# A mixture-of-experts kernel whose results are added to the output's rows by accumulating scatters instead of being gathered at the end

## The chip, the core and the metric

The kernel runs on one core of a Trainium2 chip. The core has five engines that run side by side and are ordered by semaphores: TensorE (matmuls), VectorE, ScalarE, GpSimd and SyncE, which here only issues transfers. Sixteen DMA engines move the data. Transfers issued by SyncE and ScalarE go through a hardware queue; transfers with a list of row numbers ("indirect" transfers) are issued by GpSimd, whose own program writes their descriptions.

The metric is the time of one execution on the device, in microseconds. Before the change the median of three runs is 848.52 us (847.52 to 849.83).

## What is computed

The input is 32 batches of 256 tokens with 128 numbers each, 8192 rows in all. Each row is normalised; the result goes through a causal attention of 16 heads of 8 numbers, with projection, residual and a second normalisation, and through a mixture of 8 experts, of which each token uses its best two. Both results are added to the input.

```python
def ffn(x, Wr, W1, b1, W2, b2):              # E = 8 experts, D = 128, H = 512, K = 2
    probs = softmax(einsum('bsd,ed->bse', x, Wr))
    topv, topi = top_k(probs, 2)
    combine = sum(topv[..., None] * one_hot(topi, 8), axis=2)
    for each expert e:
        h = gelu(x @ W1[e] + b1[e])
        out += combine[..., e] * (h @ W2[e] + b2[e])
    return out

xn = layernorm(x)
result = x + attention(xn, w_qkv, w_proj, b_proj, gamma, beta) + ffn(xn, Wr, W1, b1, W2, b2)
```

## The kernel before the change

The 8192 rows are held as `NT = 64` tiles of 128 rows in `x_all`; two tiles are one batch. The program has four parts.

**The beginning.** The input is loaded, its moments are computed, each row is normalised into `xn_rows`, and the router's scores are formed. VectorE picks two experts for each row and computes a slot for each of the two picks: the picks are sorted by expert, each expert's run is padded to a multiple of `S = 256` slots, and there are `NS = 72` tiles of 256 slots. A slot row in the scratch tensor `x_slots` holds the 128 numbers of the normalised row and a few extra columns: the weights, the first expert's number, and the row of the result. Slots that stay empty hold a row number far out of range (`NOWHERE`).

**The attention steps.** Batches run through a pipeline of five stages (PROJECT, MAXIMA, SOFT, FINISH, LAST); step `s` works on batch `s` in the first stage, on `s - 1` in the second, and so on, so there are 36 steps. The table `USES` gives the order of the work within a step, and each engine follows it in its own program. Most steps run in a hardware loop of two steps per pass; the last ones are written out, since they also load and convert the weights of the experts (`pieces`, L416). What matters here is SyncE's order within a step: it loads the second half of a batch's queries and keys (`load_half`, L437 and L438), stores the projected queries and keys of the next batch (L462), loads that batch's first half, and, when ScalarE has made `shift_T`, writes four rows of shifts into `q_diag` (L478). Then the next step's second half follows. TensorE waits for the second half ahead of its use `m6`. GpSimd masks the probabilities and sends, a few tiles per step, the rows to their slots (`send_tile`, L572, 128 scatters of 128 rows). The last stage (`last`, L957) adds the attention's result to the batch's rows in `x_all` and raises `res_ready`.

**The expert tiles.** Each of the 72 tiles takes three steps. SyncE loads the tile's 256 slots into one of four buffers `xg` (L497). TensorE transposes them (L1236), multiplies by the first weights (L1259, `wide`) and two tiles later by the second (L1250); ScalarE applies the activation (L687) and finally multiplies the result by the token's weight into one of four buffers `y` (L714). GpSimd scatters it, two scatters of 128 rows per tile (L619), to the rows given by `dest`: pick `c` of row `t` goes to row `2t + c` of the scratch tensor `parts_dram`, rows of empty slots go to spare rows behind. `placed[k]` counts the landings of tile `k` modulo 8. ScalarE waits for the landing of the tile four back before it writes a `y` buffer again (L710), VectorE for the one eight back before it writes `dest` again (L1021). All engines but SyncE run this stage as a loop of eight tiles, with the experts of the eight packed into one register.

**The end.** When all scatters have landed (L502), SyncE loads both parts of each row, in eight chunks of 1 MB (L507); VectorE adds them to each other and to `x_all` (L1072, L1074); ScalarE's queue stores the eight chunks of the output (L740).

Of the kernel before, what the change touches and what calls it, by code (L numbers as in the profile page):

```python
# [5 lines left out]
F32 = mybir.dt.float32  # L6
# [8 lines left out]
P = 128  # L15


def attention_and_moe(nc, x, w_qkv, w_proj, b_proj, gamma, beta, w_router, w1, b1, w2, b2, out):
# [18 lines left out]
    SW = D + 5  # L37
# [6 lines left out]
    with ctx:  # L44
# [10 lines left out]
        parts_dram = nc.dram_tensor("parts_dram", [2 * B * T + NS * S, D], F32).ap()  # L55
# [101 lines left out]
        Y_BUFS, DEST_BUFS = 4, 8  # L157
        y = o_T[:, :, :].rearrange("p b (t d) -> p b t d", d=D)
        spare_row = sb("spare_row", [P, NS * 2])
        dest = sb("dest", [P, DEST_BUFS, 2], I32)  # L160
        chosen = sb("chosen", [P, DEST_BUFS, 2, 2])
        LAST_CHUNKS, PART_BUFS = 8, 4
        LC = NT // LAST_CHUNKS
        parts = xn_rows[:, :, :].rearrange("p t d -> p (t d)")[:, 0:NT * D].rearrange("p (b t d) -> p b t d", b=PART_BUFS, d=2 * D)
# [68 lines left out]
        parts_loaded = [sem(f"parts_loaded{u}") for u in range(PART_BUFS)]  # L233
        parts_added = sem("parts_added")
        out_ready = sem("out_ready")
        out_stored = sem("out_stored")
# [70 lines left out]
        def steps(eng, step, after=((), ()), first_tile=None, written_out=False):  # L307
# [3 lines left out]
            first_whole = STAGES - 1 if not written_out else TAIL  # L311
# [95 lines left out]
        def _(sp):  # L407
# [31 lines left out]

            def step(s, par):  # L440
# [39 lines left out]
            sp.wait_ge(consts, 25)  # L480
            step(0, 0)
            sp.wait_ge(consts, 28)
            steps(sp, step)


            for u in range(2):
                sp.wait_ge(sent[u], 32 * (NT // 2))
# [23 lines left out]
        def _(pool):  # L511
# [28 lines left out]
            pool.iota(xn_rows[:, :, D + 1], pattern=[[2 * P, NT]], base=0, channel_multiplier=2,  # L540
                      allow_small_or_imprecise_dtypes=True).then_inc(consts, 1)
            pool.memset(xn_rows[:, :, D + 3], 1.0).then_inc(consts, 1)
            pool.iota(minus_row[:, :], pattern=[[0, 1]], base=0, channel_multiplier=-1,
                      allow_small_or_imprecise_dtypes=True).then_inc(consts, 1)
            pool.iota(spare_row[:, :], pattern=[[P, NS * 2]], base=2 * B * T, channel_multiplier=1,
                      allow_small_or_imprecise_dtypes=True).then_inc(consts, 1)


            pool.memset(fill[:, :, :], 0.0).then_inc(consts, 1)
            pool.wait_ge(consts, 24)  # L550
            pool.memset(fill[:, :, D + 1], NOWHERE).then_inc(fill_ready, 1)
            pool.memset(q_diag[:, 0, :, :, :], 0.0).then_inc(consts, 1)
            for c, (begin, end) in enumerate(MOMENTS):
# [6 lines left out]
                elif c == 2:  # L560
                    pool.memset(v_aug[:, :, :, :, :], 0.0).then_inc(consts, 1)
                    pool.wait_ge(consts, 27)
                    pool.memset(v_aug[:, :, :, :, HD:HD + 1], 1.0).then_inc(consts, 1)
# [6 lines left out]
            def send_tile(t):  # L570
                for c in range(2):
                    pool.indirect_dma_start(out=x_slots, out_offset=bass.IndirectOffsetOnAxis(ap=slot_i[:, t, c:c + 1], axis=0),  # L572
                                            in_=xn_rows[:, t, :], in_offset=None).then_inc(sent[t % 2], 16)
# [48 lines left out]
            tiles(pool, tile, load=False)  # L622


        @block.scalar
        def _(act):
# [68 lines left out]
            def tile(s, k, experts):  # L695
# [10 lines left out]
                if second(s):  # L706
# [3 lines left out]
                    later(act, placed[before], (s - k) * 4 + (32 if k >= 2 + Y_BUFS else 0), beyond(s, 1 + Y_BUFS))  # L710
                    act.wait_ge(xg_used, s * 2 - 2)
                    act.wait_ge(y_filled, s - 1)
                    for t in range(2):
                        act.activation(y[:, of % Y_BUFS, t, :], bank[("head", "maxB")[par]][:, D * t:D * (t + 1)], ACT.Copy,  # L714
                                       scale=chosen[:, of, t, 0:1]).then_inc(y_ready, 1)
# [22 lines left out]
            for c in range(LAST_CHUNKS):  # L738
                act.wait_ge(out_ready, c + 1)
                act.dma_start(out.rearrange("b (t p) d -> p (b t) d", p=P)[:, LC * c:LC * (c + 1), :],  # L740
                              x_all[:, LC * c:LC * (c + 1), :]).then_inc(out_stored, 16)
            act.wait_ge(out_stored, 16 * LAST_CHUNKS)


        @block.vector
        def _(dve):
            V = nc.vector
            dve.wait_ge(consts, 23)
# [87 lines left out]
            def places():  # L836
# [3 lines left out]
                then(V.tensor_scalar(xn_rows[:, :, D + 4], best[:, 0, :], -1.0, float(E), ALU.mult, ALU.add))  # L840
# [165 lines left out]
            def tile(s, k, experts):  # L1006
                quad = k % 4
                par = quad % 2
                if first(s):
# [3 lines left out]
                    V.scalar_tensor_tensor(out=chosen[:, k, :, :], in0=xg[:, quad, :, D + 4:D + 5].to_broadcast([P, 2, 2]),  # L1013
# [304 lines left out]
```

## Time and profile before the change

| | |
|---|---|
| median of three runs | 848.52 us |
| the profiled execution | 851.77 us |
| its span, first to last instruction | 850.0 us |
| TensorE busy | 699.9 us (82%) |
| VectorE busy | 692.9 us (82%) |
| ScalarE busy | 525.4 us (62%) |
| GpSimd busy | 536.0 us (63%) |
| moved by the DMA engines | 93.66 MB, 110 GB/s in the mean |

The profile comes from one execution. It lists each instruction with its start and its length, the idle time ahead of it, and what ended that idle time ("<-"). "issue" stands for idle time in which the engine waited for nothing that the profile shows. PE is TensorE, DVE VectorE, ACT ScalarE, POOL GpSimd; SPq and ACTq are transfers issued by SyncE and ScalarE. A line number such as L619 is one of the kernel. The ends of matmuls are modelled, so that a busy TensorE isn't TensorE at its peak. The shares over the whole span are means over stages with different limits; the rows further down are read by stage.

### The profile page before, as it was taken

To read this page: it belongs to the slowest core of one execution; us is meant where nothing else is said; L and a number is where in the kernel's file an instruction comes from. 1 tells how busy PE (TensorE), PEld (TensorE's weight loads), DVE (VectorE), ACT (ScalarE), POOL (GpSimd) and SP (SyncE) were. 2 spreads that over 40 slices of the span, in tenths; PEclk is the share of its full clock that TensorE was granted. 3 is DMA by queue.
4 is the path that set the end of the run, shared out by engine and by line. 5 is a ranking of instruction groups with operands and counts; after the bars stand their busy time and mean duration, and the time that the engine had idled before them with its cause. 6 is when DMAs were issued, how large, how long until landed. Compare 5 with 4: busy or idle time off the path is not lost.

```text
span 850.0 us, 24989 instructions
## 1 busy us (share of the span) xinstructions
PE 699.9 (82%) x7877; PEld 518.1 (61%) x7878; DVE 692.9 (82%) x1617; ACT 525.4 (62%) x1039; POOL 536.0 (63%) x575
## 2 busy tenths in 40 slices
PE   1366579999999999999888888868999999999800
PEld 1243346666666666666655555537888889888800
DVE  5778878898999998989889999557788888888744
ACT  4541346565656565656556565537989999999800
POOL 8750456767676776767777777334767676667710
PEclk9999899999999999999999999978999999999955
DMA  8294122232323232232233432202222222222189
GB/s 220 80 400 122 64 84 94 81 111 79 114 77 111 80 111 94 94 98 90 84 127 107 139 125 78 64 7 62 84 85 80 85 88 84 82 82 82 56 266 335
DMA packets 113313, 93.66 MB, mean 110 GB/s; under 512 B 16618, under 2 KB 97650, under 8 KB 113268
## 3 DMA queue, kind: packets, MB, share of 16 engines
q1 hardware_dynamic: 95508, 70.26, 27.0%
q0 software_dynamic: 8704, 18.17, 5.9%
q10 hardware_dynamic: 9056, 4.66, 1.9%
q8 instruction: 25, 0.41, 0.2%
q14 instruction: 20, 0.16, 0.1%
HBM read 43.85 MB, written 48.93 MB: 109 GB/s over the span
## 4 chain that ended last, share of the span: by engine, by line
PE 56%; DVE 13%; issue 7%; POOL 7%; DMA 6%; ACT 5%; SPq 5%; DVEq 0%; ACTq 0%; POOLq 0%
PE wide L1259 10%; PE bank_head L1148 7%; PE wide L1113 5%; PE bank_head L1250 5%; PE bank_maxB L1250 5%; PE bank_maxA L1127 4%; PE bank_maxB L1127 3%; DMA xn_rows<-parts_dram 3%; DMA k_cat<-qk_rows 3%; DVE shift L911 3%; POOL probs L581 3%; PE bank_misc L1173 3%; SPq L478 2%; PE bank_maxB L1131 2%; PE bank_maxA L1131 2%
## 5 line engine op out<-in xcount | busy, mean ns | idle before, releaser
L581 POOL TENSOR_SCALAR_AFFINE_SELECT probs<-probs 128x512 f32<-128x512 f32 (+1 forms) x192 | 158.3, 833 | 103.6 <-ACT probs L653 102.8
L653 ACT ACTIVATE probs<-wide 128x1024 f32<-128x1024 f32 x192 | 188.8, 1018 | 47.3 <-PE wide L1117 24.5
L619 POOL DMA_INDIRECT parts_dram<-o_T,dest x144 | 161.0, 1118 | 74.7 <-issue 48.6
L572 POOL DMA_INDIRECT x_slots<-xn_rows,slot_i x128 | 127.3, 995 | 62.8 <-DVE slot_i L868 31.4
L911 DVE TENSOR_REDUCE shift<-bank_maxA 128x2 f32<-128x512 f32 (+1 forms) x192 | 132.1, 688 | 20.1 <-PE bank_maxA L1131 12.9
L911 DVE TENSOR_REDUCE shift<-bank_maxB 128x2 f32<-128x512 f32 (+1 forms) x192 | 131.5, 685 | 4.9 <-PE bank_maxB L1131 0.8
L687 ACT ACTIVATE probs<-wide,b_all 128x256 f32<-128x256 f32 x288 | 121.4, 478 | 16.8 <-PE wide L1259 10.0
L1148 PE MATMUL bank_head<-probs,v_aug 128*32 128x256 f32 (+1 forms) x2048 | 98.9, 334 | 19.1 <-POOL probs L581 18.9
L1259 PE MATMUL wide<-xgT_raw,xnT 128*128 128x256 f16 x864 | 109.2, 277 | 3.7 <-DVE xgT_raw L1020 3.6
L1003 DVE TENSOR_TENSOR probs<-probs 128x512 f16<-128x512 f32 x144 | 99.7, 692 | 5.5 <-ACT probs L693 1.1
L1127 PE MATMUL bank_maxA<-k_cat,q_diag 128*128 128x128 f16 (+1 forms) x512 | 76.2, 252 | 28.5 <-DVE shift L911 19.5
L1148 PEld LDWEIGHTS bank_head<-probs,v_aug 128*32 128x32 f32 x2048 | 60.5, 111 | 56.2 <-issue 21.4
L1259 PEld LDWEIGHTS wide<-xgT_raw,xnT 128*128 x864 | 78.8, 99 | 16.4 <-issue 4.9
L671 ACT ACTIVATE o_T<-bank_head 128x512 f32<-128x512 f32 x64 | 38.2, 597 | 73.8 <-PE bank_head L1148 73.8
L1113 PE MATMUL wide<-q_diag,k_cat 128*128 128x512 f16 x256 | 76.9, 384 | 0.0
L1127 PE MATMUL bank_maxB<-k_cat,q_diag 128*128 128x256 f16 (+1 forms) x512 | 75.5, 250 | 0.3
L1127 PEld LDWEIGHTS bank_maxA<-k_cat,q_diag 128*128 128x128 f16 x512 | 36.7, 98 | 56.2 <-DVE shift L911 34.4
L1127 PEld LDWEIGHTS bank_maxB<-k_cat,q_diag 128*128 128x128 f16 x512 | 42.2, 99 | 30.3 <-DVE shift L911 8.0
L1131 PE MATMUL bank_maxB<-mask,ident 128*128 128x256 f16 (+1 forms) x192 | 60.5, 315 | 0.0
L1131 PE MATMUL bank_maxA<-mask,ident 128*128 128x256 f16 (+1 forms) x192 | 60.4, 314 | 0.0
L1250 PE MATMUL bank_head<-xnT,probs 128*128 x864 | 55.3, 220 | 0.0
L1250 PE MATMUL bank_maxB<-xnT,probs 128*128 x864 | 55.0, 219 | 0.2 <-DVE probs L1003 0.2
(174 smaller groups left out, 1252.4 us busy)
## 6 DMA issues: line engine op xcount, KB each, us to landing
qk_rows<-split SPq DMA_DIRECT2D x32, 512.0 KB, 3.2
x_slots<-fill SPq DMA_DIRECT2D x16, 598.5 KB, 7.6
fill<-x_slots SPq DMA_DIRECT2D x72, 133.0 KB
q_diag<-qk_rows SPq DMA_DIRECT2D x256, 32.0 KB
k_cat<-qk_rows SPq DMA_DIRECT2D x64, 128.0 KB
xn_rows<-parts_dram SPq DMA_DIRECT2D x8, 1024.0 KB, 11.8
x_all<-in_x SPq DMA_DIRECT2D x8, 512.0 KB, 7.6
pieces_f<-in_w SPq DMA_DIRECT2D x8, 512.0 KB, 4.8
```

The costliest lines, as they stand in the source:

```text
L572: pool.indirect_dma_start(out=x_slots, out_offset=bass.IndirectOffsetOnAxis(ap=slot_i[:, t, c:c + 1], axis=0), in_=xn_rows[:, t, :], in_of ...
L581: pool.affine_select(out=part, in_=part, compare_op=ALU.is_ge, fill=0.0, base=0, pattern=[[0, n], [1, P]], channel_multiplier=-1).then_inc ...
L619: pool.indirect_dma_start(out=parts_dram, out_offset=bass.IndirectOffsetOnAxis(ap=dest[:, of, t:t + 1].bitcast(U32), axis=0), in_=y[:, of ...
L653: act.activation(probs[:, u, :], ps[:, :], ACT.Exp, scale=SCALE).then_inc(empty, 1)
L687: act.activation(hT[:, par, c, :], wide[par][:, S * c:S * (c + 1)], ACT.Gelu, bias=b1_all[:, bass.ds(e, 1), c:c + 1].rearrange("p a b -> p ...
L911: V.tensor_reduce(dst, ps[:, :].rearrange("p (j k) -> p j k", j=nh), axis=AX.X, op=ALU.max, negate=True).then_inc(empty, 1)
L1113: last = M(ps[:, 512 * h2:512 * (h2 + 1)], keys[:, gs[0], :], q_diag[:, par, gs[0], 2 * h2:2 * h2 + 2, :], start=True, stop=True)
L1127: M(ps[:, keys * n_:keys * (n_ + 1)], q_diag[:, 1 - par, g, j, P * qt:P * (qt + 1)], k_cat[:, 1 - par, g, 0:keys], start=(n_ == 0), stop=F ...
L1131: M(dst, ident16[:, :], mask16[:, :].rearrange("p (o k) -> p o k", o=1).to_broadcast([P, nh, P]), start=False, stop=True, skip_group_check ...
L1148: last = M(dst, v_aug[:, of, kt, J * g + j, :], p_, start=(kt == 0), stop=(kt == 1), skip_group_check=True)
L1250: last = M(results[:, D * t:D * (t + 1)], hT_parts[:, par, hp, c, P * t:P * (t + 1)], w2_parts[:, wp_, bass.ds(e_2, 1), c, :].rearrange("p ...
L1259: last = M(wide[par][:, S * c:S * (c + 1)], w1_parts[:, wp_, bass.ds(e_1, 1), P * c:P * (c + 1)].rearrange("p a d -> p (a d)"), xgT[:, par ...
```

## The change

The scratch tensor `parts_dram` and the whole end are gone. The output itself is the place where the results meet:

- In the attention steps SyncE stores each batch's finished rows of `x_all` (input plus attention) to the output, at the end of the step after the one that finished them (`begin_out`). The last two batches are stored between the first loads of the expert tiles. GpSimd waits for all 32 stores before its first scatter of results.
- GpSimd's scatters of results carry an addition: each row is added to the output's row in memory. The row number is now that of the token, and empty slots, whose number is out of bounds, are left out by the scatter's bounds check.
- Two scatters that add to the same row must not be in flight together. Within one expert no row occurs twice. So SyncE clears each tile for GpSimd: it waits until the tile's results are in `y`, and, where the tile is the first of a new expert, until the scatters of the three tiles before it have landed. Whether the expert changes is read from the packed experts by register arithmetic. SyncE issues the load of the tile five ahead before it clears a tile.
- A slot row has one extra column less (`SW = D + 4`), since row number and pick need no choice; VectorE's selection shrinks accordingly, and `dest` is a plain copy. The counts in `placed` begin at 16, since the first scatters into `x_slots` are counted there.
- SyncE's loop of attention steps begins two steps later (`in_loop = STAGES + 1`).

```diff
-    SW = D + 5
+    SW = D + 4
...
-        parts_dram = nc.dram_tensor("parts_dram", [2 * B * T + NS * S, D], F32).ap()
+        out_rows = out.rearrange("b t d -> (b t) d")
...
+            def begin_out(b):
+
+                sp.wait_ge(res_ready, b * QT + QT)
+                sp.nop(nofuse=True)
+                sp.dma_start(out[bass.ds(b, 1), :, :].rearrange("a (t p) d -> p (a t) d", p=P),
+                             x_all[:, bass.ds(b * QT, QT), :]).then_inc(out_begun, 16)
+
+            def stores(s):
+
+                return 0 <= s - 1 - LAST < B - 2 if isinstance(s, int) else True
...
                         sp.dma_start(q_diag[row:row + 1, 1 - par, :, j, :], shift_T[G * j:G * (j + 1), :]).then_inc(shift_loaded, 16)
+                if stores(s):
+                    begin_out(s - 1 - LAST)
...
-            def tile(s, k, experts):
-                quad = k % 4
-                if not first(s):
-                    return
-
+            def load_slots(s, quad):
                 later(sp, xg_used, s * 2 - 6, beyond(s, 3))
                 sp.nop(nofuse=True)
                 sp.dma_start(xg[:, quad, :, :], x_slots[bass.ds(s * S, S), :].rearrange("(t p) d -> p t d", p=P)).then_inc(xg_loaded[quad], 16)
...
-            tiles(sp, tile, load=False)
-
-            for u in range(DEST_BUFS):
-                sp.wait_ge(placed[u], 32 * (NS // DEST_BUFS))
-            both = parts_dram[0:2 * B * T, :].rearrange("(t p c) d -> p t (c d)", p=P, c=2)
-            for c in range(LAST_CHUNKS):
-                if c >= PART_BUFS:
-                    sp.wait_ge(out_ready, c - PART_BUFS + 1)
-                sp.dma_start(parts[:, c % PART_BUFS, :, :], both[:, LC * c:LC * (c + 1), :]).then_inc(parts_loaded[c % PART_BUFS], 16)
-
+            EVEN = sum((E - 1) << BITS * j for j in range(0, FIELDS - 1, 2))
+            ODD = sum((E - 1) << BITS * j for j in range(1, FIELDS - 1, 2))
+
+            def changes_at(i):
+
+                experts = experts_of(sp, i)
+                steps_up = (experts >> BITS) - (experts & (EVEN + ODD))
+                return (steps_up & EVEN) + EVEN, (steps_up & ODD) + ODD
+
+            def clear(u, i, k, changes):
+
+                sp.wait_ge(y_ready, u * 2 + 2)
+                sp.nop(nofuse=True)
+                if beyond(u, 0):
+                    bit = BITS * (k + 1)
+                    whole = (changes[k % 2] >> bit - 5 if bit > 5 else changes[k % 2] << 5 - bit) & 32
+                    for back in range(1, Y_BUFS):
+                        if beyond(u, back - 1):
+                            sp.wait_ge(placed[(k - back) % DEST_BUFS], whole + (i * 32 + (FIRST if k >= back else FIRST - 32)))
+                            sp.nop(nofuse=True)
+                sp.nop(nofuse=True).then_inc(cleared, 1)
+
+            AHEAD = 5
+            for s in range(AHEAD):
+                load_slots(s, s % 4)
+                if s in (1, 2):
+                    begin_out(B - 3 + s)
+            changes = changes_at(0)
+            for k in range(UNROLL):
+                load_slots(k + AHEAD, (k + AHEAD) % 4)
+                clear(k, 0, k, changes)
+            with sp.Fori(0, NS // UNROLL - 2) as i:
+                changes = changes_at(i + 1)
+                for k in range(UNROLL):
+                    load_slots(i * UNROLL + (UNROLL + k + AHEAD), (k + AHEAD) % 4)
+                    clear(i * UNROLL + (UNROLL + k), i + 1, k, changes)
...
-                    pool.wait_ge(y_ready, s * 2 - 2)
+                    pool.wait_ge(cleared, s - 1)
                     pool.nop(nofuse=True)
                     for t in range(2):
-                        pool.indirect_dma_start(out=parts_dram, out_offset=bass.IndirectOffsetOnAxis(ap=dest[:, of, t:t + 1].bitcast(U32), axis=0),
-                                                in_=y[:, of % Y_BUFS, t, :], in_offset=None).then_inc(placed[of], 16)
-
+                        pool.indirect_dma_start(out=out_rows, out_offset=bass.IndirectOffsetOnAxis(ap=dest[:, of, t:t + 1].bitcast(U32), axis=0),
+                                                in_=y[:, of % Y_BUFS, t, :], in_offset=None, bounds_check=B * T - 1, oob_is_err=False,
+                                                compute_op=ALU.add).then_inc(placed[of], 16)
+
+            pool.wait_ge(out_begun, 16 * B)
             tiles(pool, tile, load=False)
+            for u in range(DEST_BUFS):
+                pool.wait_ge(placed[u], 32 * (NS // DEST_BUFS) + FIRST)
...
-            for c in range(LAST_CHUNKS):
-                act.wait_ge(out_ready, c + 1)
-                act.dma_start(out.rearrange("b (t p) d -> p (b t) d", p=P)[:, LC * c:LC * (c + 1), :],
-                              x_all[:, LC * c:LC * (c + 1), :]).then_inc(out_stored, 16)
-            act.wait_ge(out_stored, 16 * LAST_CHUNKS)
...
-                    V.tensor_tensor(dest[:, k, :], chosen[:, k, :, 1], spare_row[:, bass.ds(s * 2, 2)], ALU.min).then_inc(xg_used, 1)
+                    V.tensor_copy(dest[:, k, :], xg[:, quad, :, D + 1]).then_inc(xg_used, 1)
```

## Rows read from the trace of the kernel before

**Rows 1.** Busy times by stage: stretch, length, each engine, PEclk, DMA share, GB/s.

```profile
core 0: us, PE busy (x) PEld busy (x) DVE busy (x) ACT busy (x) POOL busy (x), PEclk, DMA share, GB/s
130.00:402.00 272.00, 266.14 (x2884) 175.44 (x2883) 248.34 (x546) 168.28 (x234) 196.60 (x235) 1.00 0.29 94
580.00:802.00 222.00, 215.60 (x2793) 197.35 (x2790) 182.04 (x488) 203.07 (x559) 154.92 (x138) 1.00 0.27 82
812.00:850.00 38.00, 0.00 (x0) 0.00 (x0) 19.60 (x16) 0.00 (x0) 0.00 (x0) 0.50 1.02 331
```

**Rows 2.** The chain that ended last, near its end: start, length in us, what.

```profile
809.34 2.22 DMA parts_dram<-o_T,dest
```

**Rows 3.** Timeline of the last tiles and the end: start, length, engine, line, work.

```profile
804.16 0.63 ACT L714 ACTIVATE o_T<-bank_head,chosen 128x128 f32<-128x128 f32 x2 [0.44 <-PE bank_head L1250]
...
805.54 0.96 POOL L619 DMA_INDIRECT parts_dram<-o_T,dest  x1 [0.99 <-ACT o_T L714]
...
809.34 0.96 POOL L619 DMA_INDIRECT parts_dram<-o_T,dest  x1 [0.30 <-issue]
811.64 19.88 SPq L507 DMA_DIRECT2D xn_rows<-parts_dram  x8
...
819.99 26.82 ACTq L740 DMA_DIRECT2D out<-x_all  x8
```

**Rows 4.** Instructions on `x_slots`, SyncE's queue in the expert stage: ns min/median/max.

```profile
L497 SPq DMA_DIRECT2D fill<-x_slots x72: 368/373/1512, 546.3 to 788.2; - x72
L497 SPq MOVE fill<-x_slots x64: 29/29/29, 587.0 to 788.1; - x64
```

**Rows 5.** The chain that ended last, expert stage: the same matmuls eight tiles apart.

```profile
652.08 1.33 PE wide L1259 x12
...
677.52 1.33 PE wide L1259 x12
```

**Rows 6.** Timeline of a tile in the expert stage: GpSimd's scatters and VectorE's CAST.

```profile
795.97 0.96 POOL L619 DMA_INDIRECT parts_dram<-o_T,dest  x1 [0.44 <-issue]
...
797.23 1.30 POOL L619 DMA_INDIRECT parts_dram<-o_T,dest  x1 [0.30 <-issue]
...
797.74 0.43 DVE L1001 CAST probs<-probs 128x512 f16<-128x512 f32 x1
...
798.97 0.96 POOL L619 DMA_INDIRECT parts_dram<-o_T,dest  x1 [0.44 <-issue]
```

**Rows 7.** Groups of instructions by line: count, busy us, mean ns, idle before.

```profile
L619 POOL DMA_INDIRECT parts_dram<-o_T,dest x144 | 161.0, 1118 | 74.7 <-issue 48.6 <-ACT o_T L714 26.2
L572 POOL DMA_INDIRECT x_slots<-xn_rows,slot_i x128 | 127.3, 995 | 62.8 <-DVE slot_i L868 31.4 <-issue 31.1 <-ACT probs L653 0.3
```

**Rows 8.** Waits on SyncE's queue: who, for whom, us in total, times, longest.

```profile
SPq L496 <- DVE dest L1023: 192.4, 68, 14.6
```

**Rows 9.** Timeline of SyncE's queue in the attention steps.

```profile
305.12 2.44 SPq L478 DMA_DIRECT2D q_diag<-shift_T  x4
307.74 1.72 SPq L437 DMA_DIRECT2D q_diag<-qk_rows  x4
309.50 0.43 SPq L438 DMA_DIRECT2D k_cat<-qk_rows  x1
...
423.96 0.43 SPq L438 DMA_DIRECT2D k_cat<-qk_rows  x1
```

**Rows 10.** Timeline of TensorE in the attention steps, the matmuls of `m6`.

```profile
311.98 0.39 PE L1127 MATMUL bank_maxA<-k_cat,q_diag 128*128 128x128 f16 x4
...
426.45 0.40 PE L1127 MATMUL bank_maxA<-k_cat,q_diag 128*128 128x128 f16 x4 [1.11 <-DMA k_cat<-qk_rows]
...
443.12 0.40 PE L1127 MATMUL bank_maxA<-k_cat,q_diag 128*128 128x128 f16 x4 [1.81 <-DMA k_cat<-qk_rows]
```

**Rows 11.** Timeline of SyncE's queue in a step that also loads a weight piece.

```profile
435.79 0.44 SPq L416 DMA_DIRECT2D pieces_f<-in_w  x1
436.34 3.61 SPq L437 DMA_DIRECT2D q_diag<-qk_rows  x4
440.00 0.42 SPq L438 DMA_DIRECT2D k_cat<-qk_rows  x1
```

**Rows 12.** GpSimd's DMA queue: packets, MB, share of 16 engines' span.

```profile
q0 software_dynamic: 8704, 18.17, 5.9%
```

More of the change, by code:

```diff
@@ L157, in attention_and_moe @@
         Y_BUFS, DEST_BUFS = 4, 8
+        FIRST = 16
         y = o_T[:, :, :].rearrange("p b (t d) -> p b t d", d=D)
-        spare_row = sb("spare_row", [P, NS * 2])
         dest = sb("dest", [P, DEST_BUFS, 2], I32)
[L161 to L164, printed above, removed]
+        chosen = sb("chosen", [P, DEST_BUFS, 2])
         wide = [ctx.enter_context(nc.psum_tensor(f"wide{i}", [P, 1024], F32)) for i in range(2)]
@@ L232, in attention_and_moe @@
         placed = [sem(f"placed{u}") for u in range(DEST_BUFS)]
[L233 to L236, printed above, removed]
+        out_begun = sem("out_begun")
+        cleared = sem("cleared")
         PROJECT, MAXIMA, SOFT, FINISH, LAST = range(5)
@@ L305, in beyond, with steps @@
             return s > n if isinstance(s, int) else True
-        def steps(eng, step, after=((), ()), first_tile=None, written_out=False):
+        assert STAGES % 2 == 1
+        def steps(eng, step, after=((), ()), first_tile=None, written_out=False, in_loop=STAGES - 1):
             experts = None
-            first_whole = STAGES - 1 if not written_out else TAIL
+            first_whole = in_loop if not written_out else TAIL
             count = TAIL - first_whole
@@ L478, in step @@
                         sp.dma_start(q_diag[row:row + 1, 1 - par, :, j, :], shift_T[G * j:G * (j + 1), :]).then_inc(shift_loaded, 16)
-            sp.wait_ge(consts, 25)
+                if stores(s):
+                    begin_out(s - 1 - LAST)
+            sp.wait_ge(consts, 23)
             step(0, 0)
-            sp.wait_ge(consts, 28)
-            steps(sp, step)
+            sp.wait_ge(consts, 26)
+            steps(sp, step, in_loop=STAGES + 1)
             for u in range(2):
-                sp.wait_ge(sent[u], 32 * (NT // 2))
+                sp.wait_ge(sent[u], 32 * (NT // 2 - DEST_BUFS // 4))
+            for u in range(DEST_BUFS):
+                sp.wait_ge(placed[u], FIRST)
             sp.wait_ge(packing, EXPERTS_PACKED)
-            def tile(s, k, experts):
-                quad = k % 4
-                if not first(s):
-                    return
+            def load_slots(s, quad):
                 later(sp, xg_used, s * 2 - 6, beyond(s, 3))
@@ L510, in _ @@
+            changes = changes_at(NS // UNROLL - 1)
+            for u in range(NS - UNROLL, NS):
+                if u + AHEAD < NS:
+                    load_slots(u + AHEAD, (u + AHEAD) % 4)
+                clear(u, u // UNROLL, u % UNROLL, changes)
         @block.gpsimd
@@ L572, in send_tile @@
                     pool.indirect_dma_start(out=x_slots, out_offset=bass.IndirectOffsetOnAxis(ap=slot_i[:, t, c:c + 1], axis=0),
-                                            in_=xn_rows[:, t, :], in_offset=None).then_inc(sent[t % 2], 16)
+                                            in_=xn_rows[:, t, :], in_offset=None).then_inc(placed[2 * t + c] if t < DEST_BUFS // 2 else sent[t % 2], 16)
             def mask(s, u):
@@ L709, in tile @@
                     before = (k - 2 - Y_BUFS) % DEST_BUFS
-                    later(act, placed[before], (s - k) * 4 + (32 if k >= 2 + Y_BUFS else 0), beyond(s, 1 + Y_BUFS))
+                    later(act, placed[before], (s - k) * 4 + (32 + FIRST if k >= 2 + Y_BUFS else FIRST), beyond(s, 1 + Y_BUFS))
                     act.wait_ge(xg_used, s * 2 - 2)
@@ L747, in _ @@
             V = nc.vector
-            dve.wait_ge(consts, 23)
+            dve.wait_ge(consts, 21)
             V.tensor_reduce(is_edge[:, :], head_edge[:, :], axis=AX.X, op=ALU.max).then_inc(prep, 1)
@@ L839, in places @@
                 V.tensor_tensor(top[:, 1, :], top[:, 1, :], top[:, 0, :], ALU.subtract).then_inc(less_top, 1)
-                then(V.tensor_scalar(xn_rows[:, :, D + 4], best[:, 0, :], -1.0, float(E), ALU.mult, ALU.add))
+                then(V.tensor_scalar(xn_rows[:, :, D + 3], best[:, 0, :], -1.0, float(E), ALU.mult, ALU.add))
                 dve.wait_ge(route_counts, 1)
@@ L1066, in _ @@
             tiles(dve, tile, load=False, begun=1)
-            for c in range(LAST_CHUNKS):
-                mine = parts[:, c % PART_BUFS, :, :]
-                here = x_all[:, LC * c:LC * (c + 1), :]
-                dve.wait_ge(parts_loaded[c % PART_BUFS], 16 * (c // PART_BUFS + 1))
-                V.tensor_tensor(mine[:, :, 0:D], mine[:, :, 0:D], mine[:, :, D:2 * D], ALU.add).then_inc(parts_added, 1)
-                dve.wait_ge(parts_added, c + 1)
-                V.tensor_tensor(here, here, mine[:, :, 0:D], ALU.add).then_inc(out_ready, 1)
         @block.tensor
```

22 lines of the change are left out of this document (10 added, 12 removed).

## The prediction

> **What bounds the kernel now.** I read the busy times by stage first [rows 1]. From 130 to 402 us, the loop of attention steps, TensorE is busy for 266.14 of 272.00 us. From 580 to 802 us, the expert tiles, it is busy for 215.60 of 222.00 us, with ScalarE at 203.07 and GpSimd at 154.92. In the last 38.00 us no engine but VectorE works, and the 16 DMA engines are full (share 1.02, 331 GB/s). So there are two TensorE-bound stages and a stretch that only moves data. The chain that ended last says where the stretch begins [rows 2]: the last scatter into `parts_dram` starts at 809.34 and has landed 2.22 us later, at 811.56. After it come eight loads of the parts (L507), sixteen additions and eight stores (L740) [rows 3]. The profiled execution took 851.77 us for a span of 850.0, 3.25 us above the median of 848.52; I take differences from the trace and apply them to the median.
>
> **What is removed.** The whole end: from 811.56 to the end of the span at 850.0, 38.4 us. Nothing else runs beside it, so all of it comes off: -38.4. The small removals (one iota and one memset on GpSimd at the start, a row of 528 instead of 532 bytes, four-element VectorE operations that shrink to two elements) lie in idle time or are a few elements long; I put them at 0.
>
> **What is added at the end.** The last tile takes the same way out as now, with SyncE in between. Today its way is: ScalarE's second multiplication ends, GpSimd starts 0.75 us later (805.54 against 804.16 + 0.63 = 804.79), two scatters of 0.96 with 0.30 between them, and 1.26 us from the end of the last one's instruction to its landing [rows 2, 3]. SyncE's hop is a wait, some register arithmetic and a few nops; a register move on SyncE's queue takes 29 ns [rows 4], so about ten such instructions are 0.3 to 0.5 us: +0.4. An addition has to read the old row before it writes; the trace has no such transfer. Between nothing and the landing of a second transfer (1.26) I take 0.5. Together +0.9.
>
> **What is added in the expert stage: GpSimd's own time.** This decides the case. Eight tiles take 25.44 us on TensorE (652.08 to 677.52) [rows 5], 3.18 us per tile and 229 us for 72 tiles. GpSimd issues two scatters per tile. An undisturbed one takes 0.96 us; one that overlaps VectorE's CAST of 0.43 us takes 1.30 (797.23 and 797.74) [rows 6]; the mean over 144 is 1.118 [rows 7], with 0.30 us between two [rows 3, 6]. So GpSimd by itself needs 2 x (1.118 + 0.30) = 2.84 us per tile, 204 us for 72. It has 25 us to spare, no more.
>
> The change spends part of that on bubbles. At each of the seven changes of expert, SyncE holds the first tile until the last three have landed. GpSimd then stands still for a landing (1.26, and 0.3 more for the addition), SyncE's hop (0.4) and its own start (0.75), less the 0.30 that it would have lost anyway: 2.4 us, or 17 us for seven. That leaves 8 us. TensorE doesn't feel a single bubble: four result buffers are 4 x 3.18 = 12.7 us of play between GpSimd and ScalarE.
>
> What an accumulating scatter costs on GpSimd no row shows. The low end is the present 1.118: the scatters of 532-byte rows into `x_slots` take 0.995 in the mean, those of 512-byte rows 1.118, and 0.96 undisturbed [rows 6, 7], so its time isn't that of bytes. For the high end I let the whole instruction grow by a half (three addresses for each row where there were two): +0.48. Each 0.1 us more costs 14.4 us of GpSimd in 144 scatters. I take +0.07, near the low end, because that is the row's own price and nothing in the rows grows with what a scatter moves: 204 + 17 + 10 = 231 against 229, +2. I add +1 for the tiles by which GpSimd may be late when TensorE stops (bounds 0 and 3).
>
> The Trainium skill speaks on both sides here. "DMA: Bandwidth & Descriptors", section "Anatomy of one DMA", calls descriptor generation small and says that many descriptors can be emitted before the incremental cost shows; by it GpSimd's addition would be 0 and the sum 2 us lower. "Collectives: The Full Stack", section "The bandwidth ceiling", says that an addition in the DMA engines needs two source reads, with two source descriptors per chunk where a copy has one. That speaks against this change: if GpSimd's time follows its descriptors, it leads to the second rival below. No run so far shows which of the two holds.
>
> **SyncE's queue in the expert stage.** Loads of tiles now stand behind the hold. Before, SyncE spent 192.4 us waiting for VectorE to free a buffer [rows 8], so it has time: a load's issue takes 0.37 us and a hold about as much in a 3.18 us tile [rows 4]. Four input buffers hide a load held back by 2 to 3 us. Without that cover each change would cost its bubble, 7 x 2.4 = 17 us. VectorE and ScalarE wait on the same landings as before, eight and four tiles back. Cost 0.
>
> **What is moved into the attention stage.** Thirty of the 32 stores of a batch's rows (128 KB each) go on SyncE's queue behind the four shift transfers of a step, and ahead of the next step's loads of its second half (L437, L438). They don't wait: the rows were finished one step earlier. But SyncE is not free there. The four shift transfers end at 305.12 + 2.44 = 307.56, the loads follow at 307.74, and the last one, of `k_cat`, is issued at 309.50 [rows 9]. TensorE uses it at 311.98, 2.48 us later, with no idle time before [rows 10]. In a step where TensorE did wait for it, the distance was 2.49 us (issue at 423.96, start at 426.45, 1.11 us idle) [rows 9, 10]. So the data arrive in the very moment in which they are used: no slack. One transfer more at this place takes 0.55 us of SyncE (the weight piece at 435.79, the next issue at 436.34) [rows 11], so TensorE will be about 0.6 us later at this point, in 27 steps. In the step with that piece of 512 KB the distance grew to 443.12 - 440.00 = 3.12 us and TensorE stood idle for 1.81 [rows 10, 11]; a store of a quarter of that size will have drained behind the four slower issues. TensorE is 98% busy there, so little of a delay is won back, yet the chain also runs through other engines: between 0 and 27 x 0.65 = 18 us I take half, 27 x 0.33 = +9. The last two stores go out between the first tiles' loads and end before GpSimd's first scatter: 0.
>
> **Sum.** -38.4 + 0.9 + 2 + 1 + 9 = -25.5, or **823.0 us**.
>
> **The rivals.**
> 1. *The stores hide.* If TensorE's later waits absorb the delay, and GpSimd stays at its price, only the end and its 0.9 us count: 848.5 - 37.5 = 811. For it: GpSimd's masks end some waits in the loop. Against it: TensorE at 98%.
> 2. *GpSimd becomes the bound (the slower side).* With +0.48 per scatter, 72 x 3.80 + 17 = 290 us of GpSimd against TensorE's 229: +61 in place of +2, 882 us. Its place is the two scatters of a tile; ScalarE would wait for landings four tiles back. It decides from the point where it eats the other 27.5 us: 8 + 27.5 = 35.5 us over 144 scatters, +0.25, a mean scatter of 1.37 us. For it: GpSimd's thin reserve, the CAST that already stretches scatters by a third, the second read. Against it: a price that doesn't follow the bytes of a row.
> 3. *Between them.* +0.12 to +0.22 per scatter: +9 to +24 in place of +2, so 830 to 845.
> 4. *The additions don't keep up in the DMA engines*, so that the change is no transfer in the background at all. Now GpSimd's queue takes 5.9% of 16 engines' 850 us for 272 x 128 = 34,816 rows, 23 ns per row [rows 12]. A tile brings 16 rows per engine; 27% of 3.18 us are in use [rows 1], 2.3 us are free, 145 ns per row. At 200 ns a tile would take 0.9 us more, +63: 884 us. A factor of six is far.
>
> **How the numbers follow.** Forecast 0.48 (its own range 812 to 836), rival 1 0.05, rival 3 0.17, rival 2 0.27, rival 4 0.03. A measurement of this kernel can tell about 0.3% (2.5 us) from no change. Faster: the forecast, rival 1 and most of rival 3, with 0.68 in all. Same: 0.04, from the cases near scatters of 1.37 us. Slower: 0.28. The range runs from 811, where nothing is paid but the end, to 866, a scatter dearer by 0.37: above it lies some 0.17, below it 0.03.
>
> **What would show it.** Right: the span ends a few us after the last scatter; the scatter's mean stays below 1.2 us; eight tiles still take some 25.5 us on TensorE; TensorE shows about half a microsecond of waiting for `k_cat` in each attention step. Wrong: idle time of ScalarE before its result multiplications, released by landings of scatters; GpSimd without idle time at scatters of 1.3 us or more; an attention step as long as before. I would be wrong above all by the price of one accumulating scatter on GpSimd, which no row shows.

## The result

The changed kernel takes 902.49 us (median of 4 runs, 901.47 to 906.66) against 849.17 (847.52 to 851.39, 4 runs): 1.0635 times as long, with a 95% interval of 1.0593 to 1.0678. The forecast was 823.0 us with a range of 811 to 866, so it has the wrong sign and the time lies outside the range. What came is the second rival, 882 us there, and 20 us more.

The profiled execution spans 901.0 us, 51.0 more than before. I cut both spans at the first and the last scatter of results. The next two fences show the cuts; the columns of a timeline are start, length in us, engine, line, work, and in brackets the idle time before it and what ended it. First the kernel before, GpSimd's timeline at its first scatter of results:

```profile
582.92 1.03 POOL L619 DMA_INDIRECT parts_dram<-o_T,dest  x1 [8.35 <-ACT o_T L714]
```

The same view of the changed kernel: the first scatter, three around a change of expert, and the last:

```profile
598.63 1.63 POOL L655 DMA_INDIRECT out<-o_T,dest  x1 [8.42 <-SPq L528]
...
630.48 1.54 POOL L655 DMA_INDIRECT out<-o_T,dest  x1 [0.30 <-issue]
632.33 2.06 POOL L655 DMA_INDIRECT out<-o_T,dest  x1 [0.30 <-issue]
637.17 1.54 POOL L655 DMA_INDIRECT out<-o_T,dest  x1 [2.78 <-SPq L528]
...
893.76 1.54 POOL L655 DMA_INDIRECT out<-o_T,dest  x1 [0.30 <-issue]
```

| stretch (by the two traces) | before, us | after, us | difference | predicted |
|---|---|---|---|---|
| start to first scatter of results | 582.92 | 598.63 | +15.7 | +9.4 |
| first scatter to end of last one | 227.4 | 296.7 | +69.3 | +3 |
| end of last scatter to end of span | 39.7 | 5.7 | -34.0 | -37.9 |

(Before, the last scatter ends at 809.34 + 0.96 = 810.30 [rows 3]; after, at 893.76 + 1.54 = 895.30.) The large term is the middle one, and it is GpSimd's. The groups of instructions by line show it (count, busy us, mean ns of one, then the idle time before them and what ended it), with the scatters into `x_slots`, which carry no addition, beside them:

```profile
L655 POOL DMA_INDIRECT out<-o_T,dest x144 | 235.8, 1637 | 69.3 <-issue 40.9 <-SPq L528 28.5
L608 POOL DMA_INDIRECT x_slots<-xn_rows,slot_i x128 | 127.3, 995 | 63.5 <-DVE slot_i L902 31.3 <-issue 31.3 <-ACT probs L693 0.9
```

The result's scatters went from 1118 ns in the mean [rows 7] to 1637; those into `x_slots` kept their 995 to the nanosecond. And nothing else is in the stage: 235.8 busy and 69.3 idle, less the 8.42 ahead of the first one, are 296.7 us, the whole stretch. Who waits for whom has turned round (waits: who, for what, us in all, times, longest):

```profile
ACT o_T L754 <- DMA out<-o_T,dest: 51.6, 52, 3.0
PE bank_maxA L1153 <- DMA k_cat<-qk_rows: 24.5, 27, 1.6
PE bank_misc L1262 <- DMA fill<-x_slots: 13.7, 5, 3.2
PE bank_maxA L1262 <- DMA fill<-x_slots: 9.0, 3, 3.2
```

ScalarE now waits 52 times for a scatter's landing before it may overwrite a result buffer. VectorE stands behind ScalarE, and TensorE behind VectorE:

```profile
DVE xgT_raw L1054 <- ACT xgT_raw L742: 69.1, 71, 2.7
PE wide L1285 <- DVE xgT_raw L1054: 28.1, 35, 2.4
```

In the stage's window (stretch, length, then busy us of TensorE, its weight loads, VectorE, ScalarE and GpSimd, granted clock, DMA share, GB/s) GpSimd is busy for 162.01 us though its scatters begin only at 598.63 (before, 154.92 [rows 1]), while TensorE's share has fallen from 97% to 82%; the attention window has lost 13.1 us of TensorE's work:

```profile
130.00:402.00 272.00, 253.01 (x2712) 166.32 (x2714) 234.64 (x515) 159.21 (x222) 186.31 (x221) 1.00 0.31 97
580.00:802.00 222.00, 182.05 (x2173) 159.14 (x2170) 143.83 (x391) 156.99 (x428) 162.01 (x99) 0.95 0.45 63
```

### The profile page after: what moved, and what is told of

It is laid out like the page before. It is cut to its first block, busy times and chain, and to the rows that moved or that the text cites. A ratio compares the mean times of both kernels' runs of the same rounds, so it can differ in the third digit from the quotient of the medians.

```text
span 901.0 us, 25844 instructions
## 1 busy us (share of the span) xinstructions
PE 714.0 (79%) x7876; PEld 523.3 (58%) x7878; DVE 673.5 (75%) x1601; ACT 524.9 (58%) x1039; POOL 611.8 (68%) x573
## 3 DMA queue, kind: packets, MB, share of 16 engines
q0 software_dynamic: 24832, 17.07, 13.1%
HBM read 35.39 MB, written 48.79 MB: 93 GB/s over the span
## 4 chain that ended last, share of the span: by engine, by line
PE 25%; issue 19%; POOL 17%; SPq 15%; DMA 11%; DVE 9%; ACT 3%; POOLq 1%; ACTq 0%; DVEq 0%
POOL out L655 14%; DMA k_cat<-qk_rows 7%; SPq L487 7%; SPq L435 5%; PE bank_head L1174 5%; PE wide L1139 3%; PE bank_maxA L1153 3%; DMA out<-o_T,dest 3%; PE bank_maxB L1153 3%; PE bank_misc L1199 2%; PE bank_maxA L1157 2%; PE bank_maxB L1157 2%; PE wide L1143 2%; SPq L442 1%; DVE xn_rows L789 1%
## 5 line engine op out<-in xcount | busy, mean ns | idle before, releaser
L655 POOL DMA_INDIRECT out<-o_T,dest x144 | 235.8, 1637 | 69.3 <-issue 40.9
L1285 PE MATMUL wide<-xgT_raw,xnT 128*128 128x256 f16 x864 | 113.0, 283 | 29.4 <-DVE xgT_raw L1054 28.1
L1153 PE MATMUL bank_maxA<-k_cat,q_diag 128*128 128x128 f16 (+1 forms) x512 | 76.4, 252 | 46.0 <-DMA k_cat<-qk_rows 24.5
L1174 PE MATMUL bank_head<-probs,v_aug 128*32 128x256 f32 (+1 forms) x2048 | 96.9, 329 | 17.2 <-POOL probs L617 17.0
L1285 PEld LDWEIGHTS wide<-xgT_raw,xnT 128*128 x864 | 81.3, 101 | 50.0 <-issue 37.6
L1174 PEld LDWEIGHTS bank_head<-probs,v_aug 128*32 128x32 f32 x2048 | 59.4, 110 | 53.7 <-issue 18.3
L1276 PE MATMUL bank_maxB<-xnT,probs 128*128 x864 | 57.5, 224 | 1.7 <-DVE probs L1037 1.7
```

The source lines that it names most:

```text
L655: pool.indirect_dma_start(out=out_rows, out_offset=bass.IndirectOffsetOnAxis(ap=dest[:, of, t:t + 1].bitcast(U32), axis=0), in_=y[:, of % ...
L1153: M(ps[:, keys * n_:keys * (n_ + 1)], q_diag[:, 1 - par, g, j, P * qt:P * (qt + 1)], k_cat[:, 1 - par, g, 0:keys], start=(n_ == 0), stop=F ...
L1174: last = M(dst, v_aug[:, of, kt, J * g + j, :], p_, start=(kt == 0), stop=(kt == 1), skip_group_check=True)
L1276: last = M(results[:, D * t:D * (t + 1)], hT_parts[:, par, hp, c, P * t:P * (t + 1)], w2_parts[:, wp_, bass.ds(e_2, 1), c, :].rearrange("p ...
L1285: last = M(wide[par][:, S * c:S * (c + 1)], w1_parts[:, wp_, bass.ds(e_1, 1), P * c:P * (c + 1)].rearrange("p a d -> p (a d)"), xgT[:, par ...
```

## The experiments

The theory after the result: an addition costs GpSimd about half a microsecond per scatter as a fixed price, and 72 tiles of two such scatters take longer than TensorE's work. Its rivals: the price goes with the rows or bytes; it comes from the bounds check that the change also adds; it comes from two additions that meet in one row; the stage is long because of the holds at the changes of expert; or the DMA engines are too slow. Beside it stands the attention stage, which I blame on the place of the stores in SyncE's queue.

**A price list.** The kernel before, in which the two scatters of a tile take one of eight forms by the tile's number modulo 8, each on its own line: plain with 128 rows (L637) and 64 (L639), with the addition 128 (L641) and 64 (L643), with a bounds check plain (L645) and adding (L647), and with rows of half the length adding (L649) and plain (L651).

```
 for t in range(2):
-    pool.indirect_dma_start(out=parts_dram, ..., in_=y[:, of % Y_BUFS, t, :], in_offset=None)
+    if of == 0:
+        i_ = pool.indirect_dma_start(out=parts_dram, out_offset=rows(t, P), in_=y[:, of % Y_BUFS, t, :], in_offset=None)
+    elif of == 1:
+        i_ = pool.indirect_dma_start(out=parts_dram, out_offset=rows(t, P // 2), in_=y[0:P // 2, of % Y_BUFS, t, :], in_offset=None)
+    elif of == 2:
+        i_ = pool.indirect_dma_start(out=parts_dram, out_offset=rows(t, P), in_=y[:, of % Y_BUFS, t, :], in_offset=None, compute_op=ALU.add)
...
```

> The kernel before, in which the two scatters of a tile take one of eight forms by the tile's number modulo 8: plain with 128 rows, plain with 64 rows, add with 128, add with 64, plain with a bounds check, add with a bounds check, add with half-length rows, plain with half-length rows. The scatters of 64 rows and of half rows leave parts of the expert results out, and the scratch is zeroed first, so its total time says nothing. Theory 'the addition costs GpSimd time': the undisturbed add of 128 rows takes 1.54 us against 0.96, with or without bounds check, and the price falls with the number of rows, not with their length (64 rows: plain about 0.7, add about 1.0). Rival 'the bounds check costs it': plain with bounds check 1.54, add without it 0.96. If the price were one of bytes, add with half rows would be near 1.25.

Its instructions by line (duration ns min/median/max, first and last start, what ended the idle time):

```profile
L637 POOL DMA_INDIRECT parts_dram<-o_T,dest x18: 955/973/1418, 642.9 to 858.3; - x18
L639 POOL DMA_INDIRECT parts_dram<-o_T,dest x18: 893/897/1381, 645.6 to 860.8; - x18
L641 POOL DMA_INDIRECT parts_dram<-o_T,dest x18: 1577/1630/2013, 648.8 to 864.0; - x18
L643 POOL DMA_INDIRECT parts_dram<-o_T,dest x18: 1422/1430/1718, 652.7 to 868.0; - x18
L645 POOL DMA_INDIRECT parts_dram<-o_T,dest x18: 1012/1040/1329, 656.4 to 871.1; - x18
L647 POOL DMA_INDIRECT parts_dram<-o_T,dest x18: 1566/1581/1804, 659.1 to 874.3; - x18
L649 POOL DMA_INDIRECT half_dram<-o_T,dest x18: 1555/1634/1974, 663.2 to 878.0; - x18
L651 POOL DMA_INDIRECT half_dram<-o_T,dest x18: 975/992/1507, 667.4 to 881.2; - x18
```

By the shortest ones, the addition costs 1422 - 893 = 529 ns on 64 rows and 1577 - 955 = 622 ns on 128: mostly a price of the instruction, not of its rows. A plain scatter is 62 ns cheaper with half the rows, an adding one 155. Rows of half the length save nothing (1555 against 1577, and 975 against 955), and the bounds check costs 57 ns without the addition and nothing with it (1566). I had expected the price to fall with the rows, and that was a miss: it hardly does. The bounds check is out as the cause. What GpSimd does in the added time no view shows.

**The change without its additions.** One argument is dropped, so the second of a token's results overwrites what the row held; holds, stores and SyncE's clearing stay.

```
-        ..., oob_is_err=False, compute_op=ALU.add).then_inc(placed[of], 16)
+        ..., oob_is_err=False).then_inc(placed[of], 16)
```

> The changed kernel with plain scatters in place of adding ones, all else kept: bounds check, holds at a new expert, SyncE's clearing, stores in the attention steps. The last expert's result of a row overwrites the rest, so the sum is left out. Theory 'the addition's price on GpSimd': scatters fall back to 1.1 us in the mean, the expert stage is TensorE's again (some 230 us from the first scatter to the last, where it was 297), and the kernel takes about 835 us. Rival 'holds and clearing by SyncE': the stage stays above 270 us and the kernel above 875.

Measured: 836.85 us, 0.9846 times before (0.9821 to 0.9871), 65.6 below the changed kernel. Its scatters by line, and the last of them in GpSimd's timeline:

```profile
L655 POOL DMA_INDIRECT out<-o_T,dest x144 | 145.3, 1009 | 90.7 <-SPq L528 55.1 <-issue 35.6
```

```profile
826.23 0.97 POOL L655 DMA_INDIRECT out<-o_T,dest  x1 [0.30 <-issue]
```

The first starts at 599.73, so the stage is 826.23 + 0.97 - 599.73 = 227.5 us: as long as before, with all holds, all clearing by SyncE, and all loads behind the holds. Among the waits there is none of ScalarE for a landing any more. So the 69 us go with the additions, and the holds cost nothing as long as GpSimd has time. The mean is also the better measure of the addition's price in this kernel: 1637 - 1009 = 628 ns, close to the 622 of the price list. The kernel before had 1118 because 60 of its 144 scatters took over 1.2 us (the one in [rows 6] overlaps a CAST); here it is 10 of 144, so the change takes 0.11 us off a scatter on one side and puts 0.63 on it on the other.

**The stores elsewhere in SyncE's queue.** The changed kernel, complete, but a batch's store goes out after the loads of the step's first half instead of after the shift transfers.

```
     load_half(s, par, 0)
+    if stores(s):
+        begin_out(s - 1 - LAST)
     ...
     (shift transfers)
-    if stores(s):
-        begin_out(s - 1 - LAST)
```

> The changed kernel with the store of a batch's finished rows issued after the first-half loads of a step, where SyncE waits 3 us per step for the shifts, instead of ahead of the second-half loads. Theory 'place in SyncE's queue': the attention steps fall from 14.8 us back to some 14.0, the first scatter of results comes at about 584 instead of 598.6, the kernel takes about 888 us. Rival 'the 4 MB of traffic themselves': steps stay at 14.8 and the kernel at 902.

Measured: 886.87 us, 1.0430 times before (1.0403 to 1.0458; the kernel before had a median of 851.0 us beside this run, against 849.17 in the result); 15.6 us are back. SyncE's queue in the changed kernel, then with the stores moved, and TensorE's wait in the kernel before and with the stores moved:

```profile
299.91 2.48 SPq L487 DMA_DIRECT2D q_diag<-shift_T  x4
302.88 0.42 SPq L442 DMA_DIRECT2D out<-x_all  x1
303.99 1.73 SPq L435 DMA_DIRECT2D q_diag<-qk_rows  x4
305.76 0.45 SPq L436 DMA_DIRECT2D k_cat<-qk_rows  x1
```

```profile
302.96 0.42 SPq L442 DMA_DIRECT2D out<-x_all  x1
305.71 2.48 SPq L489 DMA_DIRECT2D q_diag<-shift_T  x4
308.38 1.75 SPq L435 DMA_DIRECT2D q_diag<-qk_rows  x4
```

```profile
PE bank_maxA L1127 <- DMA k_cat<-qk_rows: 7.1, 7, 1.8
```

```profile
PE bank_maxA L1153 <- DMA k_cat<-qk_rows: 10.1, 14, 1.7
```

With the store between them the loads follow the end of the shift transfers (299.91 + 2.48) by 1.60 us in this step, without it by 0.19 (before, 0.18 [rows 9]). The gaps differ from step to step, and this is a large one: over the steps between 100 and 540 us the mean is 1.12 us, against 0.38 before and 0.40 with the stores moved. TensorE's wait fell from 24.5 us to 10.1, near the 7.1 that it had before the change. The first scatter starts at 585.54, so 13.1 of the 15.7 us come from the place of the stores. The other 2.6 aren't shown to have a cause: five kernels here that differ little ahead of their first scatter (the changed kernel, and the edits here that leave the stores where they are) start it anywhere from 598.63 to 602.72. The spans differ by 16.1; the other 3.0 are in the scatter stage, whose scatters took 1617 ns in the mean here, and these runs show no cause for that.

**Both edits together.** No additions, stores moved: what the end alone is worth.

> Both: plain scatters (the sum is left out) and the stores moved. If the two causes are separate and complete, the attention stage is that of before, the expert stage too, and the end is gone: 849 - 38 + 5 = 816 us. If holds or SyncE's queue cost something of their own, it shows here as the rest: with seven bubbles on the path it would be about 835.

Measured: 819.22 us, 0.9641 times before (0.9613 to 0.9668). The stage is 227.4 us again (582.50 to 809.94), and the span ends 5.3 us behind it. Its first scatter starts 17.2 us ahead of that of the run without additions, and as early as in the kernel before (582.92), SyncE's hop included. The saving at the end is therefore real, and it is what the two costs have to be set against: 17.6 us for the stores' place (836.85 less 819.22) and 68 for the additions (886.87 less 819.22).

**Each scatter in rows of its own, with and without the holds.** The additions go to rows of a scratch tensor that no other scatter touches, so that no two can meet and no hold is needed; the sums of a token are left out.

```
-        out_rows = out.rearrange("b t d -> (b t) d")
+        out_rows = nc.dram_tensor("sums", [NS * S, D], F32).ap()
...
-        V.tensor_copy(dest[:, k, :], xg[:, quad, :, D + 1])
+        V.tensor_copy(dest[:, k, :], own_row[:, bass.ds(s * 2, 2)])
...          (only in the second of the two)
-                if beyond(u, 0):
+                if False:
```

> The changed kernel with every slot added to a row of its own in a scratch tensor (the row numbers come from an iota; the expert results are left out of the output), holds at a new expert kept. It is the partner of the next run. Both theories: as the changed kernel, 902 us within 5 us, scatters of 1.64 us in the mean.

> The same with SyncE clearing a tile as soon as its results are ready, without the holds (each slot has its own row, so none is needed; the expert results are left out of the output). If GpSimd's own time sets the stage, it loses just the idle time at seven changes of expert, 7 x 2.85 = 20 us: 882 us, and GpSimd runs through at 2 x 1.94 us per tile, 280 us for the stage. If the holds and the loads held back behind them were the bound, it would fall to the 835 us of the run without additions.

Measured: 906.36 us (1.0674, 1.0642 to 1.0707) with the holds, 890.95 (1.0480, 1.0445 to 1.0514) without. The scatters by line, of the one and of the other:

```profile
L659 POOL DMA_INDIRECT sums<-o_T,dest x144 | 235.4, 1635 | 69.0 <-issue 40.5 <-SPq L530 28.2 <-DMA sums<-o_T,dest 0.3
```

```profile
L659 POOL DMA_INDIRECT sums<-o_T,dest x144 | 236.6, 1643 | 52.1 <-issue 41.8 <-SPq L530 10.0 <-DMA sums<-o_T,dest 0.3
```

1635 and 1643 ns against 1637: that additions meet in a row plays no part. The holds take the stage from 280.2 us (602.72 to 882.93) to 296.1 (600.88 to 896.97), 15.9 us for seven. The time without them missed the expected 882 by 9: 4 of these its partner with holds has too, half of them already ahead of the first scatter, and the other 5 are that the two lie 15.4 us apart where seven whole bubbles, 20 us, were expected; 2 of those 5 are the 0.30 between two scatters, which stays. The expected stage of 280 us was met. Even without a hold the stage is 53 us longer than before, so the holds are the smaller part.

**Additions in a quarter of the tiles.** Only tiles 0 and 4 of each eight add, 36 scatters of 144; the others overwrite. This asks whether GpSimd's time is free up to a point, or whether each addition costs.

```
-        compute_op=ALU.add).then_inc(placed[of], 16)
+        **({"compute_op": ALU.add} if of % 4 == 0 else {})).then_inc(placed[of], 16)
```

> The changed kernel with additions in two tiles of each eight, 36 scatters of 144, the others plain (so the sums are left out), everything else kept. If a reserve of GpSimd is what decides, 36 x 0.6 = 22 us more than the run without additions must vanish in it: 837 us, as without any addition. If each addition costs the kernel its price wherever it stands, it would be 837 + 0.25 x 66 = 853 us.

Measured: 846.30 us (0.9957, 0.9937 to 0.9977), between the two expectations.

```profile
L655 POOL DMA_INDIRECT out<-o_T,dest x144 | 177.3, 1231 | 69.3 <-issue 37.4 <-SPq L528 31.9
```

The mean rose by 222 ns, 32 us over 144, and the stage by 10.3 (599.90 to 837.66, 237.8 us): 22 us were swallowed. That is a reserve with an end. The expectation went wrong in the mean: its 22 us for the additions are there (the 36 adding scatters took 1.644 us in the mean), but the 108 plain ones took 1.092 in place of 1.009, 9 us more, since 25 of them were over 1.2 us. With 22 us alone, GpSimd's 144 x (1.009 + 0.30) + 17 = 205.5 would have come to 228, still inside TensorE's 229. It needs 144 x (1.231 + 0.30) + 17 = 237.5 us here, 8.5 above it. Why more of the plain ones are long again these runs don't separate.

This sum is the prediction's own; only the mean is put in anew, and it can be held against six kernels: the longer of TensorE's 229 us and 144 x (mean + 0.30) + 17 for the holds.

| kernel | mean scatter, ns | by the sum, us | stage measured, us |
|---|---|---|---|
| changed kernel | 1637 | 295.9 | 296.7 |
| stores moved | 1617 | 293.0 | 293.7 |
| rows of its own, holds | 1635 | 295.6 | 296.1 |
| rows of its own, no holds | 1643 | 279.8 | 280.2 |
| a quarter adds | 1231 | 237.5 | 237.8 |
| no additions | 1009 | 205.5, so 229 | 227.5 |

All six are met within 1.5 us. Where GpSimd's term is the longer one the mean comes from the same trace as the stage, so what the sum tests there is that gaps and holds are all that is added to GpSimd's own work. The bound moves from TensorE to GpSimd where the two terms meet, at a mean of 1.17 us. The point at which the whole change breaks even, 1.37 us in the prediction, comes out at 1.29 with the measured terms: the stage may grow by 34.0 - 15.7 = 18.3, to 245.7 us. The quarter with its 1.23 lies on the near side of it, just below the kernel before (ratio 0.9957).

**What would beat both.** None of these kernels that computes everything does. With all additions GpSimd needs 293 us, and moving the stores, the best that I found for the rest, leaves 887.

## Why the prediction was wrong, point by point

**The step that failed** is the price of an accumulating scatter: "I take +0.07, near the low end, because that is the row's own price and nothing in the rows grows with what a scatter moves". It was +0.52 in the mean (1118 to 1637), beyond even the high end of +0.48, or 75 us in place of 10; the addition itself cost 0.63, of which 0.11 came back because fewer scatters were stretched. The observation was right and stayed right: a row of half the length costs the same, half the rows cost little less. The inference was not. That a time doesn't follow the bytes says that it belongs to the instruction; it says nothing on how large it is for an instruction of another kind. The rows held only plain scatters, so they spoke for neither end; and the point at which the verdict turns lay between the two ends. Taking the end that the rows happened to show made a forecast out of a missing row. The chance of 0.27 for the second rival, against 0.48, has the same fault.

**The second rival** was right in its mechanism, its place and its witness. It named ScalarE's waits for landings four tiles back, and they are there: 51.6 us in 52 waits. Its 290 us for GpSimd stand against 296.7. Its own reason for the price, three addresses per row where there were two, doesn't hold: a cost per address would have halved with 64 rows, and 529 of 622 ns stayed.

**The holds.** 17 us of GpSimd were predicted, 15.9 measured; a bubble is the 2.78 us seen at 637.17. That they cost nothing in time was right under its condition: without the additions the stage is 227.5 us with all seven. With GpSimd as the bound they come out in full.

**SyncE's queue in the expert stage**, put at 0: right while GpSimd has time, by the same 227.5 us. In the changed kernel the loads do come late; TensorE stood idle for them for up to 3.2 us, 22.7 us in eight waits, so the four input buffers didn't hide every hold. This lies beside GpSimd's longer work and isn't a cost of its own there: GpSimd's sum gives the whole stage.

**The stores in the attention stage.** The place and the kind were right: the wait for `k_cat` grew from 7.1 us in 7 steps to 24.5 in 27, that is by 17.4 us, 0.64 us for each of the 27 steps. The term that was mis-sized is the halving, "between 0 and 27 x 0.65 = 18 us I take half". By the first scatters the place of the stores cost 13.1 us with the additions and 17.2 without, by the medians 15.6 and 17.6: most of the upper end, in place of 9. The 0.65 itself was a little low, 1.12 - 0.38 = 0.74 in the mean. The argument for giving half back was that the chain also runs through other engines. That TensorE, 98% busy, had no slack in which this could show is the likely reason against it, argued here and not shown; the prediction had said so itself against its first rival.

**The end.** 38.4 us were to go and 0.5 to come for the addition's landing (the hop of 0.4 is counted with the first scatter); the gain was 34.0 in the place of 37.9. The landing was sized rightly: 3.4 us from issue to landing in the median, 1.54 of them the instruction, so 1.86 behind it against 1.26 + 0.5. The other 3.8 us between the last landing and the end of the span are there without additions too (5.3 us behind the last scatter with both edits); what fills them no view shows, and it stays open.

**The DMA engines**, the last rival, were not the bound. The changed kernel's queue of GpSimd (packets, MB, share of 16 engines), and under it the same without additions:

```profile
q0 software_dynamic: 24832, 17.07, 13.1%
```

```profile
q0 software_dynamic: 8704, 17.06, 5.7%
```

The share times 16 engines and span is 1889 us against 759; the 128 scatters into `x_slots` are 759 x 128 / 272 = 357 of either, so the 16,384 added rows take 1532 us, some 93 ns each, against the 23 of [rows 12]. That is four times as much and still below the 145 ns that the prediction counted as free; in the stage's window the DMA engines are 0.45 busy.

**Set against the sum**, by terms: the expert stage 66 us more than forecast, 65 of them the additions; the way to the first scatter 6 more; the end 4 less gained. Together 76.5, which takes 823 to 899.5; the medians lie 53.3 us apart where the two profiled executions lie 51.1.

## What to carry to other kernels

An instruction of a kind that the trace doesn't hold has no price by its nearest relative: where the verdict turns on it, the case is open until a price list of one run is made, with the size and the option varied separately. Count the reserve of the engine that gets the extra work as the bound's time less the sum of its instructions, gaps and new waits; that sum held here within 1.5 us, and an edit is free up to it. Take the mean from the kernel as changed: the plain scatters' own mean was 1.12 us in the kernel before, 1.01 without additions and 1.09 beside additions in a quarter of the tiles. And a transfer put ahead of a load that arrives just in time costs most of its delay in every step (here 0.64 us of added waiting for 0.74 of delay); put where the queue isn't awaited, the same transfer left the first scatter at 582.50 to 585.54 us, against 582.92 before.

## What the hardware showed that I had not expected

- An accumulating scatter holds GpSimd 0.53 us longer on 64 rows and 0.62 on 128, whatever the length of the rows. A plain one took 0.89 and 0.96.
- In the DMA engines the adding scatter makes (24832 - 128 x 32) / 144 = 144 packets where a plain one makes 32, and takes 93 ns per row where that takes 23. The Trainium skill, "Collectives: The Full Stack", section "The bandwidth ceiling", speaks of two source reads for the addition of a ReduceScatter; this trace has more than four times the packets, and its bytes read from memory are 35.39 MB with the additions and without, so a second read doesn't show in them. "DMA: Bandwidth & Descriptors", section "Anatomy of one DMA", calls descriptor generation small. By the price list that holds for more rows (62 ns for 64 of them) and not for the addition.
- A bounds check cost GpSimd 0.06 us at most in the price list, where it leaves no row out. In the run without additions, where it leaves the empty slots out, the median scatter took 0.97 us against 0.96 before.
